# Column sums of Wq by additions and one product of minus ones, and raw turned x from tile 3 on, in a fused attention and expert kernel

## What is computed

```python
h = layernorm(x)                       # mean and variance over 512 columns
q = rope(h @ Wq)                       # 32 heads of 16
k, v = rope(ctx @ Wk), ctx @ Wv        # 8 heads of 16, each for 4 q heads
x = x + softmax(q @ k.T / 4) @ v @ Wo  # within a sequence
h = layernorm(x)
gate = softmax over the top 16 of 64 of (h @ Wr.T) @ keys.T
x = x + 2 * ((h @ A.T) * gate) @ B.T   # 64 experts of rank 8
```

## Time and profile before

| | |
|---|---|
| median of 3 runs | 168.08 us (167.92 to 168.69) |
| profiled execution | 168.37 us, span of the trace 166.7 us |
| TensorE busy | 160.6 us (96%) |
| VectorE busy | 135.0 us (81%) |
| ScalarE busy | 95.8 us (57%) |
| GpSimd busy | 87.9 us (53%) |
| granted TensorE clock | full in all 40 slices |
| moved by DMA | 18.45 MB |

### The profile page before, as it was taken

One profiled execution on the slowest core, in us unless ns is written; L12 is line 12 of the kernel. 1 busy time (PEld: TensorE's weight loads), 2 busy tenths in 40 slices (PEclk: granted clock), 3 DMA queues, 4 the chain that ended last, 5 costly groups with the idle time before them and its releaser, 6 DMA issues.

```text
span 166.7 us, 4195 instructions
## 1 busy us (share of the span) xinstructions
PE 160.6 (96%) x1437; PEld 128.9 (77%) x1437; DVE 135.0 (81%) x394; ACT 95.8 (57%) x216; POOL 87.9 (53%) x114
## 2 busy tenths in 40 slices
PE   7899999899999999999999999999999999999993
PEld 2557786777878787879887987979898877779883
DVE  2959895995998899699888998799886997867562
ACT  3588989899657453942678138832487254414210
POOL 6469999899889843724942098106321204411200
PEclk9999999999999999999999999999999999999999
DMA  5999961303315234415442263114410001000013
GB/s 118 403 402 387 409 198 67 132 6 120 98 32 159 49 79 110 117 46 172 114 112 66 93 163 94 49 49 144 109 64 4 4 0 65 0 6 0 0 63 126
DMA packets 12116, 18.45 MB, mean 111 GB/s; under 512 B 2496, under 2 KB 5056, under 8 KB 11840
## 3 DMA queue, kind: packets, MB, share of 16 engines
q1 hardware_dynamic: 11808, 17.93, 34.9%
q10 hardware_dynamic: 288, 0.27, 0.5%
HBM read 11.11 MB, written 2.10 MB: 79 GB/s over the span
## 4 chain that ended last, share of the span: by engine, by line
PE 81%; DVE 9%; issue 3%; DMA 3%; ACT 2%; ACTq 0%; DVEq 0%
PE ps_w L1342 12%; PE ps_w L1343 11%; PE ps_w L1347 11%; PE ps_t L1355 6%; PE ps_s L1426 4%; PE ps_w L1335 3%; PE ps_w L1337 3%; PE ps_w L1336 3%; DVE ps_s L1029 3%; DMA cT_in<-cT 3%; PE ps_t L1496 2%; PE ps_w L1559 2%; PE ps_t L1347 2%; PE ps_t L1343 2%; PE ps_t L1342 2%
## 5 line engine op out<-in xcount | busy, mean ns | idle before, releaser
L483 POOL TENSOR_TENSOR late<-late,gate 128x512 f32<-128x512 f32 x7 | 7.6, 1084 | 31.5 <-issue 15.0
L698 ACT ACTIVATE eT<-ps_s 128x512 f32<-128x512 f32 x32 | 17.0, 601 | 2.5 <-PE ps_s L1485 1.6
L1342 PE MATMUL ps_w<-am_hi,x2T_hi 128*128 128x288 f32 x48 | 13.8, 310 | 0.3 <-ACT x2T_hi L719 0.2
L468 POOL TENSOR_TENSOR oT_lo<-o_n,oT_hi 128x512 fp32r<-128x512 f32 x8 | 10.4, 1294 | 6.6 <-ACT oT_hi L706 6.6
L1343 PE MATMUL ps_w<-am_lo,x2T_hi 128*128 128x288 f32 x48 | 13.1, 296 | 0.0
L1342 PE MATMUL ps_w<-b_hi,zT_hi 128*128 128x512 f32 (+1 forms) x28 | 11.0, 398 | 0.0
L1019 DVE TENSOR_REDUCE ps_s<-ps_s 128x8 f32<-128x512 f32 x16 | 10.6, 688 | 0.3 <-PE ps_s L1426 0.2
L1029 DVE TENSOR_REDUCE ps_s<-ps_s 128x8 f32<-128x512 f32 x16 | 10.4, 692 | 0.5 <-PE ps_s L1445 0.3
L1335 PE MATMUL ps_w<-wq_hi,xT_hi 128*128 128x512 f32 x26 | 10.8, 414 | 0.0
L414 POOL TENSOR_TENSOR rstd<-ve,neg_half 128x1 f32<-128x1 f32 x8 | 4.4, 554 | 11.8 <-DVE ve L947 10.5
L1343 PE MATMUL ps_w<-b_lo,zT_hi 128*128 128x512 f32 (+1 forms) x28 | 10.4, 378 | 0.0
(11 more groups left out here) (280 smaller groups left out, 549.5 us busy)
## 6 DMA issues: line engine op xcount, KB each, us to landing
x_sb<-x SPq DMA_DIRECT2D x8, 256.0 KB, 6.2
q_stack<-qT_hi SPq DMA_DIRECT2D x32, 64.0 KB, 2.0
cT_in<-cT SPq DMA_DIRECT2D x7, 256.0 KB, 3.1
out<-res SPq DMA_DIRECT2D x7, 256.0 KB, 2.3
wq_sb<-wq SPq DMA_DIRECT2D x4, 256.0 KB, 5.1
late<-wo SPq DMA_DIRECT2D x1, 1024.0 KB, 7.5
am_sb<-aT SPq DMA_DIRECT2D x1, 1024.0 KB, 8.3
b_sb<-bT SPq DMA_DIRECT2D x1, 1024.0 KB, 6.7
```

The source lines that it names most:

```text
L468: pool.tensor_tensor(oT_lo[:], o_n[:].rearrange("p (b r q) -> p r b q", b=2, r=REP), oT_hi[:].bitcast(F32), ALU.subtract).then_inc(oT_lo_o ...
L698: act.activation(eT[:, c].rearrange("p b n -> p (b n)"), ps_s[:, c, :], ACT.Exp)\
L1342: pe.matmul(dst, hi(k), w_hi[:, k, cols], start=(k == 0), stop=False)
```

## The change

DIRECT goes from 4 to 3, so that tile 3 is loaded turned and raw, and its normalisation, turns and shift are gone; its rotation gets the correction. Its load stands in the queue behind c 3 and ahead of B, and waits for the first q projection. Its low part stays on VectorE and reads xT_raw (SBUF).

The four loads of Wq transposed, their passes and turns are gone. VectorE adds the four chunks of wq_sb into res: the first addition in first() behind the statistics of tile 1, the other two in second() behind rotate_k(2). TensorE multiplies a 128 x 128 tile of minus ones (set by GpSimd) with res, one float32 product of 512 columns, behind the scores of tile 1. ScalarE copies the bank behind tile 2's value blocks, ahead of c_high(3).

Tile 2's turned k goes to ps_t0 instead of ps_t1, so TensorE waits for q 1's low part before turn_k(2). In step(1) VectorE splits the maxima ahead of k's low part, and makes the residual ahead of x2's low part and of q's rotation. TensorE turns the maxima between the two halves of the output product's low part.

```diff
-DIRECT = 4
+DIRECT = 3
@@ kT_bank
-        return (ps_t1 if t < FIRST else ps_t0)[:, 0:P]
+        return (ps_t1 if t < FIRST - 1 else ps_t0)[:, 0:P]
@@ SyncE
         def load_xT(t):
             if t == DIRECT:
-                sp.wait_ge(wq_sum_ok, 1)
+                sp.wait_ge(q_ps, 1)
...
         load_x(3)
         load_c(3)
+        load_xT(3)
         sp.dma_start(b_sb[:], bT).then_inc(ld_b, 16)
         load_x(4)
         load_x(5)
-        load_wqT(0)
-        load_wqT(1)
         load_c(4)
-        load_wqT(2)
-        load_wqT(3)
@@ GpSimd
+        pool.memset(neg_ones[:], -1.0).then_inc(ones_ok, 1)
@@ ScalarE, second()
             q_high(1)
-            normalise(3)
...
             o_high(0)
             value_blocks(2)
+            sums_out()
             c_high(3)
@@ ScalarE, step(i)
                 x2_centre(g)
-                wq_sum(0)
-                wq_sum(1)
             q_high(n)
-            if f < 0:
-                wq_sum(2)
-                wq_sum(3)
...
             m_out(n)
-            if f < 0:
-                sums_out()
@@ VectorE
         def x_low(t):
             dve.wait_ge(x_hi_ok, t - RAW_Q + 1)
-            dve.tensor_tensor(xT_lo[:], xhT_bank(t)[:].rearrange("p (k q) -> p k q", k=DK),
-                              xT_hi[:].bitcast(F32), ALU.subtract).then_inc(x_lo_ok, 1)
+            raw = xhT_bank(t)[:].rearrange("p (k q) -> p k q", k=DK) if t < DIRECT else xT_raw[:]
+            dve.tensor_tensor(xT_lo[:], raw, xT_hi[:].bitcast(F32), ALU.subtract).then_inc(x_lo_ok, 1)
+
+        def add_wq(n):
+            for k in (n, n - 1) if n == 1 else (n,):
+                dve.wait_ge(ld_wq[k], 16)
+            if n > 1:
+                dve.wait_ge(wq_added, n - 1)
+            dve.tensor_tensor(res[:], wq_sb[:, 0, :] if n == 1 else res[:], wq_sb[:, n, :], ALU.add)\
+               .then_inc(wq_added, 1)
@@ VectorE, first() and second()
             statistics1(1)
+            add_wq(1)
             dve.wait_ge(q_ps, 1)
...
             rotate_k(2)
+            add_wq(2)
+            add_wq(3)
             q_low(1)
@@ VectorE, step(i)
             top(n, 1)
-            k_low(p)
             if f < 0:
                 m_parts(n)
+                k_low(p)
+                residual(i)
                 x2_low(g)
                 rotate_q(p)
             else:
+                k_low(p)
                 m_parts(n)
                 z_low(f)
-            residual(i)
+                residual(i)
             statistics2(i)
@@ TensorE
         def sum_columns():
-            pe.wait_ge(wq_sum_ok, DK)
-            for k in range(DK):
-                mm = pe.transpose(SUMS[:, P * k:P * (k + 1)], sums[:, k:k + 1].broadcast_to([P, P]), ident[:])
-            mm.then_inc(sums_ps, 1)
+            pe.wait_ge(ones_ok, 1)
+            pe.wait_ge(wq_added, DK - 1)
+            pe.matmul(SUMS, neg_ones[:], res[:], start=True, stop=True).then_inc(sums_ps, 1)
@@ TensorE, second()
             project_q(2, [2])
+            pe.wait_ge(qT_lo_ok, 2)
             turn_k(2)
             project_q(2, [3]).then_inc(q_ps, 1)
-            pe.wait_ge(qT_lo_ok, 2)
-            turn_xh(3)
             scores(1, 0)
             scores(1, 1)
+            sum_columns()
@@ TensorE, step(i), end
-            project_out(i)
+            out_high(i)
             if f >= 0:
+                out_low(i)
                 pe.wait_ge(q_rot, 2 * p + 2)
                 up_high(f)
-            turn_m(n)
-            if f >= 0:
+                turn_m(n)
                 up_low(f)
                 turn_q(p)
             else:
-                pe.wait_ge(x2T_lo_ok, i)
-                sum_columns()
+                out_low_part(i, [0, 1])
+                turn_m(n)
+                out_low_part(i, [2, 3]).then_inc(y_ps, 1)
```

More of the change, by code:

```diff
@@ L55, with build @@
 PI_LOW = float(np.nextafter(np.float32(np.pi), np.float32(0)))
-def build(nc, x, xT, cT, pos, wq, wqT, wkv, wo, aT, router, bT, out):
+def build(nc, x, xT, cT, pos, wq, wkv, wo, aT, router, bT, out):
     ctx = ExitStack()
@@ L109, in build @@
         cs, cs_q = sb("cs", [P, T, 2 * HD]), sb("cs_q", [P, 2 * HD])
-        sums = sb("sums", [P, DK])
+        neg_ones = sb("neg_ones", [P, P])
         bn1, mv1, ve1 = sb("bn1", [P, 6]), sb("mv1", [P, 2]), sb("ve1", [P, 1])
@@ L194, in build @@
         SUMS = ps_t1[:]
-        def wqT_of(k):
-            return (xT_raw[:].rearrange("p k q -> p (k q)"), res[:], z_sb, zg)[k]
         def inv_of(t):
@@ L245, in build @@
         ld_wkv = [sem(f"ld_wkv{half}") for half in range(2)]
-        wq_sum_ok, sums_ps, sums_ok = (sem(n) for n in ("wq_sum_ok", "sums_ps", "sums_ok"))
-        ld_wqT = [sem(f"ld_wqT{k}") for k in range(DK)]
+        ones_ok, wq_added, sums_ps, sums_ok = (sem(n) for n in ("ones_ok", "wq_added", "sums_ps", "sums_ok"))
         cs_q_ok, q_mean_ok = sem("cs_q_ok"), sem("q_mean_ok")
@@ L295, in load_xT @@
                 sp.dma_start(xT_raw[:], xT[t]).then_inc(ld_xT[t], 16)
[L297 to L302, removed]
             def load_c(t):
@@ L416, in deviation1 @@
                     pool.wait_ge(rstd1_ok, t + 1)
-                    pool.wait_ge(q_rot, 2 * t)
+                    if t > DIRECT:
+                        pool.wait_ge(q_rot, 2 * t)
                     pool.tensor_scalar(cs_q[:], cs[:, t, :], rstd1[:], None, ALU.mult).then_inc(cs_q_ok, 1)
@@ L550, in step @@
                 f, n, p = i - 2, i + 1, i + 2
-                if p >= DIRECT:
+                if p > FIRST:
                     deviation1(p)
@@ L632, in x_high @@
                 act.activation(xT_hi[:], raw, ACT.Copy).then_inc(x_hi_ok, 1)
[L634 to L637, removed]
             def sums_out():
@@ L1158, in result @@
                 if t == 0:
-                    dve.wait_ge(wq_sum_ok, 2)
+                    dve.wait_ge(sums_ps, 1)
                 else:
@@ L1806 @@
         "wq": np.asarray(L0_xattn_Wq).reshape(DK, P, D),
-        "wqT": rows(np.asarray(L0_xattn_Wq).T),
         "wkv": halves(np.concatenate([np.asarray(L0_xattn_Wk), np.asarray(L0_xattn_Wv)], axis=1)),
```

## The result

The changed kernel takes 169.84 us (median of 9 runs, 169.09 to 170.63) against 168.08 of the kernel before on the same chip: a ratio of 1.010, 95% interval 1.0072 to 1.0128, some 1.7 us. 169.3 was forecast, with a range from 167.6 to 170.5. Its profiled execution took 169.1 us (span 167.4), one of the shorter of the nine. Tables of after name other lines than before: the same functions stand some 10 to 25 lines further up.

The account below looks back on a forecast made before the run. VectorE and TensorE, both busy nearly all the time from 39.3 to 68.6 us, were taken as the bound. The sums' copy 0.53 plus 0.67 by tile step 2 gave +1.2 us: 169.3 against 168.08, range 167.6 to 170.5.

Parts of the forecast that it names:

- What is removed is worth nothing: Tile 3's turns and normalisation, and the sums' loads and passes, gain 0; the sums' turns free 0.74 us of TensorE.
- The additions cost nothing: VectorE's three additions, about 0.6 us each, fit into idle gaps before 12.09 and 26.74: 0, ends 0 and +1.1.
- The sums' copy, +0.53: The copy in ScalarE's gapless run moves tile 1's maxima by 0.5 us and its turned scores to 35.22.
- inside it: TensorE's own +0.25 us for the product was taken as contained in the copy's +0.53.
- The low part of x 3, taken as 0: VectorE's low part now reads SBUF twice; 0.7 us before the projection covers a wait: 0, ends 0 and +0.7.
- Step 1: Tile step 1: tile 2's turned scores win 0.48 us; VectorE's residual idles 0.75, correction takes 0.75; TensorE ends 0.1 later.
- Step 2: Tile step 2: VectorE is 1.5 us later with 0.8 slack; TensorE's turn of k 4 moves +0.67 beyond the transpose's shift.
- From there on the shift stays: From 68.6 us on nothing of the program changes, so a shift that stands at 61 us stays.
- The port: Rival, 0.15: the second or third addition waits behind a GpSimd subtraction, q 1's low part starts 1.07 later: 170.4 us.
- Given back: Rival, 0.17: in step 2 the selection misses GpSimd's subtractions and VectorE regains about 0.6 us: 168.7 us.
- TensorE alone decides: Rival, 0.15: TensorE's stream is the bound, loses 0.52 and 0.74 and gains 0.9, -0.36 us: 167.7 us.
- wrong would be turned scores at 34.7: Sign against the forecast: turned scores of tile 1 starting at 34.7 instead of about 0.5 us later.

Follow-up runs that it names:

- e4: The kernel before with only the sums changed to three additions and one product, tile 3 still normalised and turned: 168.41 us, ratio 1.0006.
- e3: The changed kernel without the second and third addition of Wq's chunks: 169.56 us, ratio 1.0087.
- e1: The changed kernel with ScalarE's copy of the sums moved behind the exponentials of tile 1: 169.49 us, ratio 1.0091.
- e9: The kernel of e7 with the loads of tile 3's stacked keys ahead of x 7 and turned x 5 in SyncE's queue: 168.22 us, ratio 1.0023.
- e2: The changed kernel with x2's low part put ahead of the residual on VectorE in step(1): 168.83 us, ratio 1.0043.
- e6: The changed kernel without the correction by the mean for tile 3: 169.03 us, ratio 1.0052.
- e7: The kernel of e5 with tile 4's statistics made in second(), with two buffers for mean and variance: 168.89 us, ratio 1.0039.
- e5: The changed kernel with the edits of e1 and e2 together: 168.93 us, ratio 1.0046.

## Why the prediction was right

The direction and the main chain of causes came out as forecast: slower, at 1.67 us where 1.2 were summed. The sum was low by 0.4 to 0.5, and the measured median lies near the upper end of the forecast's own range (168.9 to 169.9). Its terms in order:

- **What is removed is worth nothing.** Right as far as tested: e4 shows no gain from the loads and passes of the sums (ratio 1.0006). The turns of normalised tile 3 weren't tested alone, but the row at 29.40 agrees: the second half of the scores still waits for VectorE's division.
- **The additions cost nothing.** Right for 2 and 3 (e3). Wrong by 0.2 for the first: its idle time on VectorE was read, but not who runs beside it. GpSimd's power for tile 1's deviation ran there and became 0.44 us longer, GpSimd stayed late, and TensorE's turn of normalised tile 2 with it. The stated end of +1.1 was wide enough, but it was meant for waits of additions 2 and 3.
- **The sums' copy, +0.53.** It stands where it was said to, and without it TensorE starts the scores unheld (e1). From tile 0's turned scores to tile 1's the shift is 0.65 (0.86 less 0.21): the spacing was 0.63 instead of 0.5, which is the whole of the difference. But only 0.38 belongs to the copy; TensorE's 0.25 for the product stands by itself once the copy is gone, which "inside it" had said.
- **The low part of x 3, taken as 0.** Right in the changed kernel: 1.04 us, hidden. Its bound of 0.7 was needed in e9, where 0.40 came through.
- **Step 1.** The turned scores of tile 2 won 0.33 us relative to tile 1's, not 0.48, and q 4's projection stands 0.29 late, not 0.11. Both come from one term, the place of the maxima's split. VectorE's transpose is 0.11 later in this trace (39.45 against 39.34), so the split should have ended at 46.84, and it ended at 46.98. The prediction let it start where k's low part had stood, 2.53 us behind the start of the last four reductions; but it reads their result and starts 2.66 behind them (43.71, 46.37). k's low part had filled that gap. TensorE waited 0.22 us for it (row at 47.04), and the residual stands at 47.98 instead of 47.78. From the residual to q 4's projection the steps were right to 0.01 us: 3.52 against 3.53. The wait of 0.80 (0.75 said) and the correction of 0.75 (0.75 said) are there, and e2 and e6 price them with 0.45 and 0.76.
- **Step 2.** From q 4's projection to the turn of k 4, 0.46 us more than before where 0.56 was said. VectorE had used its two waits as forecast; with 1.0 us of work moved away (e7) the second one is back.
- **From there on the shift stays.** Right: 1.61 at the turn of k 4, 1.67 at the stacked scores, 1.7 in the medians.

The sum: 0.21 for the first addition, 0.12 more for the copy, 0.18 more in step 1, 0.10 less in step 2: 1.2 becomes 1.6.

**The rivals.** The port, as placed (second or third addition behind a subtraction), did not delay q 1's low part. The Trainium skill's rule (SBUF — State Buffer, section "Who interferes with whom") says that the one that comes second is blocked for the whole of the other's instruction, and the trace agrees, with numbers: it waits out what is left of it. In e9 GpSimd's subtractions end near 35.55, VectorE's low part began at 34.68 and ended at 36.13, 0.58 behind that; GpSimd's next, q_r, began at 35.55 and took 1.73 instead of 1.30. "Given back" did not happen either: e_top took 0.64 us again (0.67 in the earlier trace rows), the subtractions having moved along with the selection, as the argument against it said. "TensorE alone decides" has to be read with care: its sign was turned scores of tile 1 within 0.2 us of 34.69, and in the trace's own time they stand at 34.81; also "wrong would be turned scores at 34.7" is nearly met. Only counted from the first product are they 0.86 late. The rival fell with the 0.36 us idle before 34.81, which e1 took away, and with e2 and e6, which edit VectorE alone and give time back.

## What to carry to other kernels

Where two engines are both near full, an instruction that is put ahead of its neighbours costs the wait that it opens and not its own length. Before a residual or any other consumer is moved forward, look what has its operands already and let that go first: swapping two lines was worth about 0.5 us here, while the removal of a megabyte of loads and four passes brought nothing. And an idle gap that takes an addition with two SBUF inputs is only free if GpSimd has nothing due in it.

Count landmarks of two traces from a common event behind the first loads. The raw profiled times differed by 0.73 us, the medians by 1.76 and the landmarks by 1.67. And a wait in one trace is one execution's: before it is called the bound, see whether the transfer it names took its usual time.

## What the runs showed of the hardware

The exclusion between VectorE and GpSimd is passed on. Timelines of VectorE and of GpSimd in e9:

```profile
34.68 1.45 DVE L928 TENSOR_TENSOR xT_lo<-xT_raw,xT_hi 128x512 fp32r<-128x512 f32 x1
```

```profile
32.76 2.82 POOL L391 TENSOR_TENSOR am_lo<-am_sb,am_hi 128x576 fp32r<-128x576 f32 x2
35.55 1.73 POOL L426 TENSOR_TENSOR q_r<-q_a,q_b 128x512 f32<-128x512 f32 x1
```

The same VectorE instruction took 0.82 to 1.45 us in nine traces (1.04 after, 1.12 in e7), by how much of GpSimd's subtraction was left, and 0.68 where it reads PSUM (before and e4); and it held up the next one of GpSimd in turn. Even a power of a single column was made 0.44 us longer by a 128x512 addition. So one instruction of this kind can delay both engines, and moving unrelated work by a few tenths changes the price.

SyncE issues a load of a 32-partition block into the stacked operands every 0.63 us (0.59 us each), 12 for the keys and 12 for the queries of a tile: 15 us of issue. The DMA share of that stretch is 0.36, so it is the count of transfers and not the bytes that fills the queue. Most land 2.0 us after their issue. In most traces one issue between 55 and 61 us takes 1.1 to 1.7 us instead (1.67 in e1, 1.30 in e5), and one landing took 2.9 (e7), which made TensorE wait 0.42 us; why stays open.
